# Four moves in a chain of four blocks: one turn of tokens instead of two, a copy ahead of a norm, products taken in pairs, and a group's sums taken earlier

## The reference

```
block 0: conv = BN(depthwise 13x13) + BN(depthwise 3x3) + BN(x);  ffn = 4 experts, 2 chosen per token
block 1: conv = cascaded attention over six heads;                ffn = 4 experts
block 2: value, query, key, offset = depthwise 3x3 of x           ffn = 4 experts
         offset -> layernorm over channels -> GELU -> 2 positions -> tanh
         sampled = bilinear samples of value at the positions
         out = (query^T key * scale) sampled, then a 1x1 projection
block 3: linear attention: out = m0*v + scale*q(k^T v) - diag*v, 1x1 projection, m0 a sum over everything
         ffn = quantised: W binarised in 5 groups; for each of 5 groups of 3 images:
         y = x W1 + b1;  gamma = max|y|;  h = GELU(clip(y*128/gamma));  the same again with W2
```

## Time and profile before

| | us |
|---|---|
| median of 3 runs | 1213.68 |
| lowest and highest of them | 1210.94, 1234.04 |
| the profiled execution, its own time | 1208.81 |
| its span, first to last instruction | 1207.0 |
| mean granted TensorE clock | 0.952 |
| first convolution, up to its expert stage | 0 to about 84 |
| third convolution | about 657 to 821 |
| tail of the fourth convolution and quantised layers | about 1114 to 1207 |

### The profile page before, as it was taken

The page is one execution under the profiler, slowest core; times in us unless marked ns, Lnnn a source line. Parts: engine busy times, 40 slices in busy tenths (PEclk is TensorE's granted clock), DMA queues, the critical chain, the costliest instruction groups (busy, mean ns, idle before and its releaser), DMA issues. The chain is left out here.

```text
span 1207.0 us, 24782 instructions
## 1 busy us (share of the span) xinstructions
PE 1111.6 (92%) x8774; PEld 967.2 (80%) x8774; DVE 810.0 (67%) x2904; ACT 485.6 (40%) x976; POOL 255.7 (21%) x244
## 2 busy tenths in 40 slices
PE   3979999989999999999998988889999999999776
PEld 3758999978899998899997666568999987887554
DVE  7257676756766664577776767655877767776775
ACT  3843433425555553343342324233343422332451
POOL 5013212110211000212122534342121221211110
PEclk9979999988999999899999789899999999999887
DMA  4302010010000000000001121200000000000001
GB/s 148 95 5 69 22 47 5 0 53 1 2 2 2 1 2 1 1 2 1 0 0 36 37 48 25 49 1 1 2 1 0 0 1 1 2 1 1 5 10 40
DMA packets 15246, 21.60 MB, mean 18 GB/s; under 512 B 8761, under 2 KB 10383, under 8 KB 15026
## 3 DMA queue, kind: packets, MB, share of 16 engines
q1 hardware_dynamic: 14434, 18.53, 5.2%
q10 hardware_dynamic: 720, 1.85, 0.4%
HBM read 11.59 MB, written 3.15 MB: 12 GB/s over the span
## 5 line engine op out<-in xcount | busy, mean ns | idle before, releaser
L1222 PEld LDWEIGHTS moe_dn<-all_w,moe_hid 128*128 128x128 f32 x2304 | 269.7, 192 | 6.8 <-DVEq L1116 1.5
L1222 PE MATMUL moe_dn<-all_w,moe_hid 128*128 128x96 f32 x2304 | 271.9, 275 | 1.1 <-DVEq L1116 1.1
L1163 ACT ACTIVATE moe_hid<-moe_up 128x512 f32<-128x512 f32 x288 | 169.5, 598 | 234.5 <-PE moe_up L1214 221.4
L1212 PE MATMUL moe_up<-front_xh,front_w1h 97*128 97x512 f32 x288 | 122.1, 424 | 0.6 <-PEq L1708 0.3
L1113 DVE SCALAR_TENSOR_TENSOR all_X<-moe_dn,front_gate,all_X 128x96 f32 (+1 forms) x384 | 95.3, 311 | 29.0 <-PE moe_dn L1222 23.0
L1214 PE MATMUL moe_up<-front_xl,front_w1h 97*128 97x512 f32 x288 | 113.8, 395 | 0.0
L1213 PE MATMUL moe_up<-front_xh,front_w1l 97*128 97x512 f32 x288 | 113.4, 394 | 0.0
L1105 DVE SCALAR_TENSOR_TENSOR all_X<-all_b,front_gate,all_X 128x96 f32 (+1 forms) x384 | 98.9, 319 | 5.7 <-DVE front_var L83 2.6
L1060 POOL TENSOR_TENSOR front_prob<-front_euler,front_logit 128x16 f32<-128x16 f32 x21 | 60.9, 2900 | 193.9 <-DVEq L533 193.9
L1603 PE MATMUL l1c_o<-second_vs,l1c_pt 128*128 128x64 f32 x768 | 92.8, 274 | 0.4 <-DVE l1c_ro L1413 0.4
L1603 PEld LDWEIGHTS l1c_o<-second_vs,l1c_pt 128*128 128x128 f32 x768 | 90.2, 192 | 2.7 <-issue 0.6
(11 more groups left out here) (419 smaller groups left out, 1979.9 us busy)
## 6 DMA issues: line engine op xcount, KB each, us to landing
third_st<-third_xp SPq DMA_DIRECT2D x72, 76.5 KB, 2.1
all_w<-w SPq DMA_DIRECT2D x3, 582.0 KB
all_w<-w SPq DMA_DIRECT2D x3, 576.0 KB
all_X<-x_rows SPq DMA_DIRECT2D x2, 768.0 KB, 7.1
conv_scratch<-all_X SPq DMA_DIRECT2D x2, 768.0 KB, 3.2
all_X<-conv_scratch SPq DMA_DIRECT2D x2, 768.0 KB, 4.9
out_tokens<-l3f_y SPq DMA_DIRECT2D x5, 288.0 KB, 2.1
l0c_band<-band ACTq DMA_DIRECT2D x1, 1344.0 KB, 9.7
```

What stands on the lines that cost most here:

```text
L1163: act.activation(hid[:, n, :], up[n % UPS][:, :], ACT.Gelu).then_inc(hid_done, 1)
L1212: pe.matmul(bank, w1h[:, n, :], xh[:, p, :], start=True, stop=False)
L1222: last = pe.matmul(dn[e % 2][:, j * C:(j + 1) * C], hid[:, n, j * P:(j + 1) * P], w2[:, n, :], start=(k == 0), stop=(k == KC - 1))
```

## The change

First convolution: groups 4 to 11 are turned into the lower half only and copied out once; SyncE copies the lower half of `xt` into the upper half, one element on, by a transfer per group, and issues the late weights in eight parts between these transfers (the two quantised matrices stay ahead of them). `fill` of groups 3 to 11 has three instructions on ScalarE, the fourth goes to VectorE (`fill_last`). Third convolution: VectorE copies the values out ahead of the offsets' norm, tap 5 comes behind the norm and tap 8 behind the first samples; TensorE projects both halves of a pair behind the offsets' convolution of the next step, alternating with the scores. Fourth: group 1's m0*v, sums and variances are taken in `l3_conv`, group 0's normalising behind them. Quantised layers: ScalarE normalises group 1 first and group 1 is turned ahead of `ups(0)`; group i+3's m0*v and sums go into the two waits of `factors(i+1)`, its variances behind `clip`; one piece of `ups(1)` goes between the two products of the first maximum; 24 idle products stand ahead of the last `downs`.

```diff
@@ l0_conv, SyncE
             load_weights(sp, T, A)
+            flat = xt[:, :, :, :].rearrange("p g i r -> p (g i r)")
+            each, size, count = 2 * NI * (SIDE + 1), len(LATE), NG - TWICE
+            sp.wait_ge(pads, 2)
+            for n in range(count):
+                g = TWICE + n
+                sp.wait_ge(xt_done, g + 1)
+                sp.dma_start(flat[UPPER, each * g:each * (g + 1) - 1], flat[LOWER, each * g + 1:each * (g + 1)]
+                             ).then_inc(shifted[n % 2], 16)
+                load_late(sp, T, A, size * n // count, size * (n + 1) // count)
@@ ScalarE
-                for k in range(HC):
+                for k in range(HC if g < FIRST else HC - 1):
...
-                act.activation(x[LOWER, :, 1:SIDE + 1], image[LOWER, :, :], ACT.Copy)
-                act.activation(x[UPPER, :, 0:SIDE], image[UPPER, :, :], ACT.Copy).then_inc(xt_done, 1)
+                last = act.activation(x[LOWER, :, 1:SIDE + 1], image[LOWER, :, :], ACT.Copy)
+                if g < TWICE:
+                    last = act.activation(x[UPPER, :, 0:SIDE], image[UPPER, :, :], ACT.Copy)
+                last.then_inc(xt_done, 1)
@@ VectorE
+            dve.wait_ge(band_done, 2)
             for n in range(NP):
+                if n + 3 < NG:
+                    fill_last(n + 3)
                 add_back(n)
@@ TensorE, turn and conv_piece
-                        for rows in (LOWER, UPPER):
+                        for rows in (LOWER, UPPER) if g < TWICE else (LOWER,):
...
+                if g >= FIRST:
+                    pe.wait_ge(last_done, g - FIRST + 1)
+                if g >= TWICE:
+                    pe.wait_ge(shifted[(g - TWICE) % 2], 16 * ((g - TWICE) // 2 + 1))
@@ l2_conv, VectorE
                     offset_moments(p)
-                    value_taps(p, 5, 6)
-                    offset_norm(p)
                 if live(p - 1):
                     values_out(p - 1)
+                if live(p):
+                    offset_norm(p)
+                    value_taps(p, 5, 6)
...
-                    value_taps(p, 6, TAPS)
+                    value_taps(p, 6, 8)
                 if live(p - 1):
                     sampled_out(p - 1, 0)
+                if live(p):
+                    value_taps(p, 8, TAPS)
@@ l2_conv, TensorE
                 if live(p - 2):
+                    project(p - 2, 0)
+                if live(p - 1):
+                    scores(p - 1, 0)
+                if live(p - 2):
                     project(p - 2, 1)
                 if live(p - 1):
-                    scores(p - 1, 0)
                     scores(p - 1, 1)
...
                     outputs(p - 1, 1)
-                    project(p - 1, 0)
+            project(NP - 1, 0)
             project(NP - 1, 1)
@@ l3_conv, VectorE
-            dve.wait_ge(S["y_out"], NI)
-            add_m0(NT - 2, NT)
             add_m0(TG, 2 * TG)
+            for n in range(TG, 2 * TG):
+                last = dve.bn_stats(N["stats"][:, n, :], X[:, n, :])
+            chain.sync(last)
+            variances(dve, chain, N, TG, 2 * TG)
...
@@ l3_ffn, VectorE
-            group_sums(1)
             up_maxima(0, range(MS))
             up_maximum(0)
             dve.sem_inc(S["max_done"], 1)
-            factors(0)
+            factors(0, lambda: last_term(2), lambda: group_sums(2))
             clip(0)
-            group_sums(2)
+            group_variances(2)
...
-                factors(i + 1)
+                more = i + 3 < QG
+                factors(i + 1, (lambda: last_term(i + 3)) if more else None, (lambda: group_sums(i + 3)) if more else None)
@@ ScalarE
+            normalise(1)
             tokens_out(0)
+            tokens_out(1)
@@ TensorE
             turn(0)
             pe.wait_ge(S["consts"], 1)
+            turn(1)
             ups(0)
             top_in(0)
+            ups(1, 0, 1)
             top_out(0)
-            turn(1)
+            ups(1, 1, MS)
             for i in range(QG):
-                if i + 1 < QG:
+                if 1 <= i < QG - 1:
                     ups(i + 1)
+                if i == QG - 1:
+                    stay_awake(pe, tp[0], ident, 24)
                 downs(i, 0)
```

More of the change, by code:

```diff
@@ L127, in load_weights, with load_late @@
     load_expert_weights(sp, T, A, 0)
-    for name in LATE:
+    for name in QUANT:
+        sp.dma_start(T[name][tuple(slice(None) for _ in T[name].shape)], A[name]).then_inc(T["quant_in"], 16)
+def load_late(sp, T, A, lo, hi):
+    for name in LATE[lo:hi]:
         t = T[name]
@@ L247, in l0_conv @@
                                                                     "inv_spread"))
-        dve_step, band_done, full_done, xn_done = (s.sem(n) for n in
-            ("dve_step", "band_done", "full_done", "xn_done"))
+        dve_step, band_done, full_done, last_done, xn_done = (s.sem(n) for n in
+            ("dve_step", "band_done", "full_done", "last_done", "xn_done"))
+        shifted = [s.sem(f"shifted{n}") for n in range(2)]
         turned, xt_done, conv_done, conv_out, back_done, back_out = (s.sem(n) for n in
@@ L429, in add_back, with fill_last @@
                                   ALU.add).then_inc(back_out, 1)
+            def fill_last(g):
+                if g >= RF:
+                    dve.wait_ge(conv_done, g - RF + 1)
+                k = HC - 1
+                dve.tensor_scalar(full[:, g % RF, :, :, k, :].rearrange("p a j x -> p (a j) x"),
+                                  band[:, 2 * g:2 * g + 2, :, :].rearrange("p a j x -> p (a j) x"), own[:, k:k + 1],
+                                  None, ALU.mult).then_inc(last_done, 1)
+            dve.wait_ge(band_done, 2)
             for n in range(NP):
+                if n + 3 < NG:
+                    fill_last(n + 3)
                 add_back(n)
@@ L2249, in _ @@
                     pool.wait_ge(S["consts"], 3)
-            pool.wait_ge(S["first_var"], 1)
-            pool.tensor_tensor(N["rstd"][:, 0:TG], N["var"][:, 0:TG], N["mhalf"][:, 0:TG], ALU.pow
-                               ).then_inc(S["first_rstd"], 1)
+            for n in range(2):
+                part = slice(TG * n, TG * (n + 1))
+                pool.wait_ge(S["first_var"], n + 1)
+                pool.tensor_tensor(N["rstd"][:, part], N["var"][:, part], N["mhalf"][:, part], ALU.pow
+                                   ).then_inc(S["first_rstd"], 1)
+            pool.wait_ge(S["first_rstd"], 2)
+            pool.tensor_tensor(N["shift"][:, part], N["shift"][:, part], N["rstd"][:, part], ALU.mult)
         @block.vector
@@ L2542, in _ @@
         def _(pool):
-            for g in range(1, QG):
+            for g in range(2, QG):
                 part = slice(TG * g, TG * (g + 1))
-                pool.wait_ge(S["var_done"], g)
+                pool.wait_ge(S["var_done"], g - 1)
                 pool.tensor_tensor(N["rstd"][:, part], N["var"][:, part], N["mhalf"][:, part], ALU.pow
                                    ).then_inc(S["pow_done"], 1)
-                pool.wait_ge(S["pow_done"], g)
+                pool.wait_ge(S["pow_done"], g - 1)
                 pool.tensor_tensor(N["shift"][:, part], N["shift"][:, part], N["rstd"][:, part], ALU.mult
@@ L2554, in _, with last_term, group_variances @@
             chain = Chain(dve, S["dve_step"])
+            def last_term(g):
+                lo, hi = TG * g, TG * (g + 1)
+                chain.sync(dve.scalar_tensor_tensor(out=X[:, lo:hi, :], in0=kv[:, lo:hi, VW], scalar=m0[:, 0:1],
+                                                    in1=X[:, lo:hi, :], op0=ALU.mult, op1=ALU.add))
             def group_sums(g):
-                lo, hi = TG * g, TG * (g + 1)
-                if g > 1:
-                    chain.sync(dve.scalar_tensor_tensor(out=X[:, lo:hi, :], in0=kv[:, lo:hi, VW], scalar=m0[:, 0:1],
-                                                        in1=X[:, lo:hi, :], op0=ALU.mult, op1=ALU.add))
-                for n in range(lo, hi):
+                for n in range(TG * g, TG * (g + 1)):
                     last = dve.bn_stats(N["stats"][:, n, :], X[:, n, :])
                 chain.sync(last)
+            def group_variances(g):
+                lo, hi = TG * g, TG * (g + 1)
                 variances(dve, chain, N, lo, hi)
@@ L2588, in results, with factors @@
                 chain.sync(dve.tensor_reduce(bmax[:, 1:2], yf, AX.X, ALU.max, apply_absolute_value=True))
-            def factors(f):
+            def factors(f, first_wait=None, second_wait=None):
+                if first_wait:
+                    first_wait()
                 wait(dve, S["max_in"], f + 1)
@@ L2650, in normalise @@
             def normalise(g):
-                wait(act, S["rstd_done"], g)
+                wait(act, S["rstd_done"], g - 1)
                 wait(act, S["turned"], g - 1)
@@ L2705, in turn, with ups @@
                 ins.then_inc(S["turned"], 1)
-            def ups(g):
+            def ups(g, lo=0, hi=MS):
                 wait(pe, S["xt_done"], g + 1)
-                for m in range(MS):
```

(5 more changed lines are left out.)

22 lines of the change are left out of this document (15 added, 7 removed).

## The result

The change makes the kernel slower by 0.6%: 1216.24 us against 1210.64 us (medians of 20 runs each), a ratio of 1.0061 with a 95% interval of 1.0042 to 1.0080. I had forecast 1204, 9 us faster. The profiled execution after has a span of 1216.0 us, 9.0 more than before. The page's part 1 stands against the earlier trace rows: TensorE is busy 8 us longer, with 16 records fewer.

The account below looks back on a forecast made before the run. It took TensorE's work, waits and clock to bound the kernel, with a chain of engines in the quantised layers. First convolution +6.7, third -15, fourth's end and quantised layers -1 gave -9: median 1213.7 to 1204, range 1191 to 1218.

Parts of the forecast that it names:

- the clock's part of the third convolution: Third convolution: fewer waits per step bring back half of the 2 us a step lost to the clock, 6 us gained.
- The structural gain: Third convolution: the new order shortens a full-clock step from about 18.0 to 16.7 us, 9 us gained over 7 steps.
- My tap 8 term: Third convolution: with tap 8 behind the first samples, `sample(p-1, 1)` comes about 1.0 to 1.3 us earlier.
- The first shift: First convolution: `conv_piece(4)` waits for group 4's transfer, held behind one engine's queued loads; a loss of 4.1 us.
- ScalarE's relief: First convolution's start: one fill fewer on ScalarE shortens the chain ahead of the turn back, 0.4 us gained.
- The clock behind that wait: First convolution: TensorE's clock falls behind the wait for the first shift; a loss of 3 us.
- Turning once: First convolution: halving a turn's products saves 0, since the two output halves already run side by side.
- the shifts of the steady loop hidden: First convolution's loop: a transfer of about 2.6 us fits into 3.6 us of slack, so it costs nothing.
- Rival 1: First convolution: late weights make the shift late at every step, 11 us more, the kernel at 1222; chance 0.13.
- rival 2: First convolution: turning once saves its 3.9 us and the first shift lands early, the kernel at 1194; chance 0.15.
- Quantised layers, -0.7: Fourth convolution's end and quantised layers: chain to `ups(4)` +0.7, idle products -1.4, sum -0.7 us.
- Rival 3: Third convolution: only the projection's wait is gained and the clock falls as before; total 0, the kernel at 1214; chance 0.22.

Follow-up runs that it names:

- t_old_idle: The kernel before with 8 idle products of TensorE ahead of `sample(p-1, 1)`; ratio to the kernel before 1.0049.
- t_dve_idle: The kernel before with VectorE's new order in the third convolution, TensorE's old order, and 8 idle products ahead of `sample(p-1, 1)`; ratio 1.0043.
- t_pe_idle: The kernel before with TensorE's new order in the third convolution, VectorE's old order, and 8 idle products ahead of `sample(p-1, 1)`; ratio 0.9900.
- f_lower2: The changed kernel with 97-row matrices loaded as 96 and 1 rows, and groups 4 to 11 turned twice into the same lower half; ratio 1.0008.
- s_rows96: The changed kernel with each matrix of 97 rows loaded as 96 rows and 1 row; ratio to the kernel before 0.9988.
- b_split_idle: The changed kernel with 97-row matrices loaded as 96 and 1 rows, and 8 idle products ahead of `sample(p-1, 1)`; ratio to the kernel before 0.9939.
- p3_quant: The kernel before with only the change's part in the fourth convolution's end and the quantised layers; ratio 0.9992.
- t_idle: The kernel before with the third convolution's part alone and 8 idle products ahead of `sample(p-1, 1)`; ratio 0.9913.

## Why the prediction was wrong

Forecast -9, profiled +9.0 (+5.6 by the medians): 18 us off between the profiled executions, of which the third convolution is 13.5, the first 4.2, the quantised layers 0.8.

- **The step that failed: "The waits per step fall from over 3 us to 1.5, so I book half of it back, 7 x 0.9 = 6", the clock's part of the third convolution.** I priced the low clock by the sum of the waits. t_old_idle and t_dve_idle show that the sum says little: with a single wait of 0.87 us in a step of 23.9 the clock falls in five and in four steps in a row. In the changed kernel two short waits went and the long one stayed, and windows at 0.60 and 0.78 came. Before, 1 - clock times the length of each of the seven windows behind 668.5 gives 18 us; after, from 679.0, 23: the clock took 5 us more instead of giving 6 back. These 11 are most of the 13.5. Both are estimates from one execution each; in the others of the new order the third convolution took 159.3 to 176.3 us, 6 less to 11 more than the 165.1 before, so the clock's part is different each time and in none the forecast's. My bounds of -6 and -22 left out that the clock could get worse.
- **The structural gain, -9: right in kind, sized too large.** A step at the full clock went from 18.2 or 18.4 to 17.4, not from 18.0 to 16.7: 6 to 7 us instead of 9, by an estimate of 0.8 to 1.0 a step. The wait ahead of `sample(p-1, 1)` stayed at 2.05 where I had followed both engines to 1.5. The waits of 0.88 and 0.69 did go. My tap 8 term is bounded by t_pe_idle: all of VectorE's new order gives 0.4 of the 1.0 to 1.3.
- **The first shift, +4.1: right cause, half the size** (8.6), which with the clock behind it puts the first convolution at +10.9, outside my bounds of +1.8 and +8. SyncE's 39.7 was measured as 39.59. The engine's queue ran nearer 25 GB/s (24 and 25 in the windows above, where it is alone) than the 27 of the window that I used: by that estimate 803 kB from 12.9 end at 45.0, not 42.7. Behind it I allowed 1.5 us for the shift, which needs at least the 2.3 of the others; and the weights issued behind it, which I had only as a rival for the steady loop, cost 1.3. ScalarE's relief, -0.4, came: the wait of 1.48 ahead of the turn back is 1.16 in the changed kernel.
- **The clock behind that wait, +3:** measured 2.4.
- **Turning once, 0, the shifts of the steady loop hidden, VectorE's fills hidden:** shown by f_lower2 and by the step of 3.91. Rival 1 (late at every step) and the saving in rival 2 didn't come; what rival 1 named, late weights ahead of a shift, shows at one step of s_rows96 (0.50 us) and b_split_idle (1.66).
- **Quantised layers, -0.7:** measured -0.2, and in part by luck. The start of `ups(0)` (+4.5) and the idle products (1.6 against 1.4) fit; the low clock in `ups(0)` was 1.1 here (5.56 against 4.50), 2.0 in p3_quant, against 3. Up to `ups(4)` the stage was 1.6 us longer (61.1 against 59.5) where I had 0.7. So behind `ups(0)` the moved work gave back 4.0 us net (4.5 + 1.1 - 1.6), not the 6.8 of my sum (4.5 + 3 - 0.7), and a smaller clock loss hid it.
- Rival 3, which I gave 0.22, was nearest: "the clock falls as before" and a sum of 0. What it lacked was the first shift's other 4.5 us and a clock that falls deeper than before.

The forecast of "within 2%" holds; the sign did not.

## What to carry to other kernels

A transfer put into a queue costs what still stands ahead of it on its slowest engine: look at the transfers' rate just before it, and if the share is a sixteenth, look for a load with a leading dimension like the 97 here and split off the remainder. For a loop of many short waits on TensorE, as the third convolution here, don't compute the clock's cost from the sum of the waits: fill the longest, remove the others by order, and check that a step at a granted clock of 1.00 repeats. Before a moved step is credited with "the clock comes back", run it once with idle products in the wait that remains; here the third convolution's part alone went from a ratio of 0.997 to 0.991 with them.

## What the hardware showed unexpectedly

- With a wait of 0.87 us as the only one in a step of 23.9, TensorE's clock fell in five steps in a row (t_old_idle, granted 0.54 over the next 15 us) and in four (t_dve_idle), to 0.71 over a whole step. Before, with four waits in a step, the steps behind 709 are at 0.85 to 0.99. But the same wait of 0.88 us brought no fall at 681.17 in t_dve_idle and in the end of t_idle. What besides the wait decides it stays open. The Trainium skill tells in TensorE: Matmul & The Clock Gate, section A second HAM failure mode: psum-queue depth-cycling, of a kernel in which frequent short idles between groups of products make the clock swing between its two levels. The 23.9 us steps agree in that the clock swings with no long wait, though they hold one short idle and not many, and no run here shows more of its rule.
- The same eight idle products don't help everywhere: in the new order they gain 0.6% (0.9972 to 0.9913, with intervals that just overlap), in the old one nothing (1.0049, 0.9999 to 1.0099), and with TensorE's old and VectorE's new order the kernel is 0.4% slower than before (1.0043, 1.0005 to 1.0081).
- Products into the two halves of output partitions ran side by side here: eight products in 1.04 us against 1.91 when all go to one half.
